# A cross-attention kernel on one core: the fourth batch's K projected ahead of V, its stack sent in halves

## What is computed

```python
Q = (query @ Wq.T + bq).reshape(B, Sq, N_HEADS, D_K).transpose(0, 2, 1, 3)
K = (key_value @ Wk.T + bk)...
V = (key_value @ Wv.T + bv)...
scores = jnp.einsum('bhqd,bhkd->bhqk', Q, K) / np.sqrt(D_K)
attn = jax.nn.softmax(scores, axis=-1)
context = jnp.einsum('bhqk,bhkd->bhqd', attn, V)
x = context @ W_o.T + b_o + query
return (x - mu) / jnp.sqrt(var + LN_EPS) * ln_gamma + ln_beta
```

## Time and profile before

| what | value |
|---|---|
| median of 3 runs | 149.05 us (148.85 to 150.97) |
| the profiled execution's own time | 149.44 us |
| its span, first to last instruction | 147.6 us |
| mean granted TensorE clock | 0.979 |
| PE busy | 131.0 us, 89% of the span |
| DVE, ACT, POOL busy | 94.0, 89.0, 82.3 us |
| DMA queue of SP (q1) | 17.36 MB, 36.9% of 16 engines |
| DMA queue of POOL (q0) | 1.70 MB, 4.6% |

### The profile page before, as it was taken

The page is one execution under the profiler, slowest core; times in us unless marked ns, Lnnn a source line. Parts: engine busy times, 40 slices in busy tenths (PEclk is TensorE's granted clock), DMA queues, the critical chain, the costliest instruction groups (busy, mean ns, idle before and its releaser), DMA issues.

```text
span 147.6 us, 3918 instructions
## 1 busy us (share of the span) xinstructions
PE 131.0 (89%) x1479; PEld 115.3 (78%) x1479; DVE 94.0 (64%) x220; ACT 89.0 (60%) x180; POOL 82.3 (56%) x101
## 2 busy tenths in 40 slices
PE   5798988799999269999999999999999999999940
PEld 4497967789889157988898989898989888778620
DVE  3466997988657333487657776877677786521432
ACT  3676445376586511957586678764867557776510
POOL 8958993984068400400429998991347007587531
PEclk9999999999999969999999999999999999999996
DMA  4996893780079896065007105641070010110111
GB/s 125 348 351 225 264 331 118 281 272 7 4 200 239 251 251 176 24 237 165 8 0 262 53 8 158 217 163 32 8 288 25 12 29 4 31 29 15 33 31 31
DMA packets 15731, 19.59 MB, mean 133 GB/s; under 512 B 2544, under 2 KB 14896, under 8 KB 15712
## 3 DMA queue, kind: packets, MB, share of 16 engines
q1 hardware_dynamic: 14656, 17.36, 36.9%
q0 software_dynamic: 592, 1.70, 4.6%
q10 hardware_dynamic: 464, 0.28, 0.6%
HBM read 6.30 MB, written 0.92 MB: 49 GB/s over the span
## 4 chain that ended last, share of the span: by engine, by line
PE 66%; SPq 14%; DMA 9%; DVE 3%; issue 2%; ACT 2%; ACTq 1%; POOLq 0%; DVEq 0%
PE m_bank L848 16%; PE st_bank L922 13%; PE pv_bank L938 13%; PE mx_bank L889 12%; SPq L259 6%; SPq L311 6%; DMA k_stack<-k_hl 5%; PE m_bank L969 4%; DMA c_raw<-ctxT 3%; PE m_bank L949 2%; DMA q_stack<-q_hl 1%; DVE mx L709 1%; PE m_bank L957 1%; PE mx_bank L922 1%; PE mx_bank L938 1%
## 5 line engine op out<-in xcount | busy, mean ns | idle before, releaser
L709 DVE TENSOR_REDUCE mx<-mx_bank 112x1 f32<-112x375 f32 x128 | 64.2, 541 | 26.1 <-PE mx_bank L889 25.9
L610 ACT ACTIVATE pw<-st_bank 125x448 f32<-125x448 f32 x90 | 47.6, 545 | 27.0 <-PE st_bank L922 26.8
L889 PE MATMUL mx_bank<-k_stack,q_stack 128*112 128x376 f32 x128 | 43.9, 356 | 6.0 <-DMA k_stack<-k_hl 4.1
L922 PE MATMUL st_bank<-q_stack,k_stack 128*125 128x224 f32 x180 | 36.3, 287 | 0.8 <-DMA q_stack<-shift_half 0.6
L922 PEld LDWEIGHTS st_bank<-q_stack,k_stack 128*125 128x125 f32 x180 | 29.8, 188 | 4.4 <-issue 2.6
L889 PEld LDWEIGHTS mx_bank<-k_stack,q_stack 128*112 128x112 f32 x128 | 22.3, 178 | 8.9 <-DMA k_stack<-k_hl 4.3
L411 POOL TENSOR_TENSOR k_hl<-k_full,k_hl 128x376 fp32r<-128x376 f32 x10 | 10.0, 999 | 25.5 <-ACT k_hl L528 25.5
L938 PE MATMUL pv_bank<-pw,v_sb 125*17 125x112 f32 x720 | 21.2, 264 | 0.0
L385 POOL TENSOR_TENSOR c_hl<-c_raw,c_hl 128x752 fp32r<-128x752 f32 x6 | 10.8, 1801 | 14.7 <-ACT c_hl L499 14.7
L938 PEld LDWEIGHTS pv_bank<-pw,v_sb 125*17 125x17 f32 x720 | 16.6, 99 | 3.1 <-issue 1.8
L848 PE MATMUL m_bank<-w_hl,c_hl 128*125 128x256 f32 x126 | 18.1, 282 | 0.0
(11 more groups left out here) (107 smaller groups left out, 170.4 us busy)
## 6 DMA issues: line engine op xcount, KB each, us to landing
k_stack<-k_hl SPq DMA_DIRECT2D x48, 188.0 KB, 2.5
c_raw<-ctxT SPq DMA_DIRECT2D x8, 375.0 KB, 3.9
q_stack<-q_hl SPq DMA_DIRECT2D x12, 112.0 KB, 2.3
q_stack<-q_hl SPq DMA_DIRECT2D x6, 168.0 KB, 3.3
x_space<-x_nat POOLq DMA_DIRECT2D x1, 896.0 KB, 11.7
out<-yo SPq DMA_DIRECT2D x8, 112.0 KB, 2.0
pw<-wT SPq DMA_DIRECT2D x2, 256.0 KB, 4.6
x_space<-xT SPq DMA_DIRECT2D x2, 224.0 KB, 5.5
```

Of the source, the lines that this page charges most:

```text
L610: nc.scalar.activation(p_tile[0:KC, n % PR, :, :], st_of(n)[0:KC, 0:4 * Q].rearrange("p (j q) -> p j q", j=4), ACT.Exp, scale=float(DK) ** ...
L709: nc.vector.tensor_reduce(mx[b % 2][:, h % 2, q_pair(h // 2):q_pair(h // 2) + 1], mx_bank[n % MR][0:Q, 0:KV], axis=AX_X, op=ALU.max, negat ...
L889: nc.tensor.matmul(mx_bank[n % MR][0:Q, 0:KVP], q_stack[k][:, side, q_pair(h // 2), b - Q_STACKS[k][0], :], k_stack[b % 3][:, h // 2, :], ...
L922: last = nc.tensor.matmul(st_of(n)[0:KC, k * 2 * Q:(k + 1) * 2 * Q], k_stack[i % 3][:, 2 * g + k, c * KC:(c + 1) * KC], q_stack[qk][:, :, ...
```

## The change

In batch 0, K of batch 3 is projected in units 2 and 4, V of batch 2 in units 5, 6 and 7, Q's third group in units 9 and 10. The taking of each by ACT and DVE moves with it, as do the orders of the PSUM banks. ACT splits context 4 in unit 8 and not in 5, and POOL does `context_lo(4)` behind the two `subtract_k`, not ahead of them. SP sends K's stack of batch 3 in batch 0: half 0 ahead of batch 1's shift, once batch 0 has done 6 units, half 1 behind the shift, once it has done 12; Q's third group follows. In batch 1, units 6 and 7 take no head for the maxima and units 8 to 11 take 1, 2, 2 and 1, where each of units 6 to 11 took one.

```diff
 U_OUT, U_OT, U_BIAS, U_Q, U_CONTEXT = 0, 6, 0, 11, 5
-U_K = ((9, 11), (8, 10))
-U_V = (2, 3, 4)
+U_K = ((2, 4), (8, 10))
+U_V = ((5, 6, 7), (2, 3, 4))
...
-FIRST_JOBS = {1: (("MT", 0, 1),), 5: (("Q", 2, 0),), 6: (("Q", 2, 1),)}
+FIRST_JOBS = {1: (("MT", 0, 1),), 9: (("Q", 2, 0),), 10: (("Q", 2, 1),)}
...
-M0_JOBS = [("K", 0, 0), ("V", 0, 0), ("Q", 1, 0), ("K", 2, 0), ("V", 2, 0), ("Q", 2, 0), ("K", 3, 0)]
-M1_JOBS = [("K", 0, 1), ("V", 0, 1), ("Q", 1, 1), ("K", 2, 1), ("MT", 0, 1), ("V", 2, 1), ("Q", 2, 1), ("MT", 1), ("K", 3, 1)]
+M0_JOBS = [("K", 0, 0), ("V", 0, 0), ("Q", 1, 0), ("K", 2, 0), ("K", 3, 0), ("V", 2, 0), ("Q", 2, 0)]
+M1_JOBS = [("K", 0, 1), ("V", 0, 1), ("Q", 1, 1), ("K", 2, 1), ("MT", 0, 1), ("K", 3, 1), ("V", 2, 1), ("MT", 1), ("Q", 2, 1)]
...
-FIRST_HEADS = ((2, 2, 2, 2, 2, 2, 2, 2, 1, 1, 1, 1), (2, 2, 2, 2, 2, 2, 1, 1, 1, 1, 1, 1))
+FIRST_HEADS = ((2, 2, 2, 2, 2, 2, 2, 2, 1, 1, 1, 1), (2, 2, 2, 2, 2, 2, 0, 0, 1, 2, 2, 1))
...
-                if b >= 3:
+                if b == 3:
+                    sp.wait_ge(st_full, HALF * (t + 1))
+                elif b > 3:
                     sp.wait_ge(st_full, UNITS * (b - 2))
...
             for i in range(B):
-                if 1 <= i < B - V_AHEAD:
+                if 2 <= i < B - V_AHEAD:
                     for t in range(2):
                         stack_k(i + V_AHEAD, t)
                 if i + AHEAD + 2 < B:
                     load_context(i + AHEAD + 2)
+                if i == 0:
+                    stack_k(AHEAD, 0)
                 if i + 1 < B:
                     stack_shift(i + 1)
+                if i == 0:
+                    stack_k(AHEAD, 1)
                 if i in (0, 3):
...
-                if i + AHEAD + 1 < B:
+                if 1 <= i and i + AHEAD + 1 < B:
                     context_lo(i + AHEAD + 1)
                 if i + AHEAD < B:
                     for t in range(2):
                         subtract_k(i + AHEAD, t)
+                if i == 0:
+                    context_lo(AHEAD + 1)
...
-                    if i + V_AHEAD < B and u in U_V[1:]:
-                        v_part(i + V_AHEAD, u - U_V[1])
-                    if i == 0 and u in (5, 6):
-                        q_hi_part(2, u - 5)
+                    if i + V_AHEAD < B and u in U_V[min(i, 1)][1:]:
+                        v_part(i + V_AHEAD, u - U_V[min(i, 1)][1])
+                    if i == 0 and u in (9, 10):
+                        q_hi_part(2, u - 9)
...
-                    if u == U_CONTEXT and i + AHEAD + 1 < B:
+                    if u == (U_CONTEXT if i else 8) and i + AHEAD + 1 < B:
                         context_hi(i + AHEAD + 1)
...
-                    if u in (6, 7) and i == 0:
-                        q_lo_part(2, u - 6)
+                    if u in (10, 11) and i == 0:
+                        q_lo_part(2, u - 10)
...
-                    if i + V_AHEAD < B and u in U_V:
-                        v_project(i + V_AHEAD, U_V.index(u))
+                    if i + V_AHEAD < B and u in U_V[min(i, 1)]:
+                        v_project(i + V_AHEAD, U_V[min(i, 1)].index(u))
```

## The result

The changed kernel takes 151.92 us (median of 20 runs, 149.91 to 155.36), the kernel before 149.21 (20 runs, 147.49 to 152.38). The ratio is 1.0159, with a 95% interval of 1.0116 to 1.0202: slower by 1.6%, where 2% faster was forecast. The time lies above the stated range. Every ratio here compares the fast executions of the two kernels, those within 1.5% of their fastest, so it differs from the quotient of the medians beside it. The profiled execution took 150.49 us with a span of 148.7, 1.1 more than before.

The account below looks back on a forecast made before the run. PE was taken to set the time from 60 us on, after a 4.11 us hole waiting for K's stack. Gain 5.65 less 0.65, less 1.85 for Q, leaves 3.15: 146.3 us profiled, median 145.9, range 143.8 to 148.3.

Parts of the forecast that it names:

- What bounds the kernel, what is bought: Batch 1, unit 6 to unit 9's first head: 4.6 us against 10.6, a gain of 5.65 if nothing makes PE wait.
- What batch 0 loses: Reordered PE work and later exponentials in batch 0 make batch 1 run 0.65 to 0.7 us later, leaving net 5.0.
- What comes late next: Q's third group now lands last: side 1 at 55.5, so head 49 in batch 1 starts there, not at 53.65.
- The bytes: SP's queue must move 1.61 MB from about 43.1, at 105 GB/s beside POOL's 149: side 1 lands at 55.8.
- The sum: Of the 5.0 us, 1.85 is given back at head 49 and 3.15 stays, with the clock priced at 0.
- C: Q's wait replaces K's and is longer, side 1 landing from 57.5 on; at 58.5 the time is 150.5 us; chance 0.06.
- B: Heads 48 and 49 wait 2.6 us or more together and the clock falls again: gain 0.8, 148.2 us; chance 0.15.
- A: Q's stack is in time, with no wait: gain 5.0, median 144.05 us; chance 0.23.
- D: Unit 0 of batch 1 or 2 waits for its shift, the latter behind context 6: 147.1 us; chance 0.08.

Follow-up runs that it names:

- e3: Changed kernel with x_nat issued in batch 1 behind context 5's low part, and Q's third group ahead of K's half 1: 146.75 us, ratio 0.985.
- e13: Changed kernel with Q's third group ahead of K's half 1 and x_nat issued in batch 2 behind context 6's low part: 145.47 us, ratio 0.978.
- e1: Changed kernel with only x_nat's load moved, to batch 1 behind the low part of context 5: 147.37 us, ratio 0.987.
- e7: The kernel of e3 with SP sending batch 2's shift ahead of context 6: ratio 1.001 to the kernel before.
- e11: Changed kernel with Q's third group ahead of K's half 1 and x_nat between batch 1's two K subtractions: 145.29 us, ratio 0.988.
- e4: Kernel before with only x_nat's load moved, to batch 1 behind the low part of context 5: 149.07 us, ratio 0.989.
- e5: Changed kernel with POOL's whole group of loads held back until unit 1 of batch 1 has its scores: ratio 1.020.
- e8: Changed kernel with POOL's group of loads moved ahead of the low part of context 4: ratio 1.031.
- e2: Changed kernel with only SP's order changed, Q's third group ahead of half 1 of K's stack: 151.77 us, ratio 1.020.
- e10: Kernel before with x_nat issued behind POOL's memset: 150.07 us, ratio 0.995.

## Why the prediction was wrong

*What bounds the kernel, what is bought.* Right, by e3 and e13: with the stack and Q in time, the hole and the half clock go. From unit 6 to the first head of unit 9 e13 takes 4.5 us (50.84 to 55.32), and 4.6 was forecast. e13's ratio of 0.978 is 3.3 us of the 5.0 that were priced for no wait at all, and its span is 3.4 below that of the kernel before. But its profiled execution was late before any of the change can act: ACT's exponential of unit 2 in batch 0, at 30.13 in the earlier trace rows, comes at 31.94. From that exponential to the end e13 is 5.2 us shorter, so the price of 5.0 was right in size, as far as one pair of profiled executions shows. Why the first 30 us differ from one execution to the next was not looked into.

*What batch 0 loses.* Right wherever it was read: PE's wait at unit 4 grew by 0.4 us, from 0.20 to 0.60, the maxima's transpose was forecast for 38.6 and came at 38.81, batch 1's unit 0 for 41.8 and came at 41.92 (41.39 before), unit 8 for 51.5 and came at 51.52. K's half 0 was issued at 33.74 (forecast 33.6) and landed by 38. Batch 1's shift took 1.8 us to land, and it did not make unit 0 wait.

*What comes late next.* Right in kind: Q's third group replaced K's stack, and POOL's loads moved forward to just the forecast times (41.99 and 44.39). The step that failed is "The bytes", with its last sentence on side 0. It gave each queue a constant rate (149 and 105 GB/s) and let Q's two sides land in proportion to the bytes ahead of them: side 1 at 55.5, side 0 "0.52 MB earlier, 51 to 53". Side 0 landed at 56.7 and side 1 at 58.7. The mean rate of SP's queue was not the error. It moved 1.69 MB between 43.1 and 56.75:

```profile
q1 hardware_dynamic: 984, 1.69, 48.2%
q0 software_dynamic: 464, 1.52, 43.8%
```

That is 124 GB/s. The forecast, 1.61 MB from 43.1 to 55.8, is 127. All of POOL's loads were moved in the same time. What was wrong is which bytes moved when, and for whom the last ones were. In 48.5 to 51.5 us it looked like this:

```profile
q0 software_dynamic: 142, 0.57, 67.4%
q1 hardware_dynamic: 61, 0.14, 13.5%
```

x_nat was being drained and Q hardly moved. Side 0's last DMA, issued 0.9 us behind x_nat, landed with side 1's, 0.8 us behind the first of them. And by 56.75 SP's queue had moved more than the 1.61 MB that the forecast counted for side 1, which landed 2 us later still: some of what moved was context 5, issued behind it. So the parts of a transfer did not finish in proportion to the bytes ahead of it. That this is a matter of how unequal the 16 engines' backlogs are is a guess, as the profile does not tell them apart. A mean rate over a window of the kernel before could not show it, as there Q had been sent with nothing of POOL ahead of it. What the earlier trace rows showed for 46 to 52.84, 60.4% against 32.2%, is a mean of two things. Mostly beside `wo` and the three rows both queues moved, 0.38 and 0.35 MB in 48 to 51 us; in 51 to 53 us, when what POOL's queue moved was mostly x_nat, SP's got little:

```profile
q0 software_dynamic: 104, 0.39, 77.5%
q1 hardware_dynamic: 88, 0.11, 19.0%
```

The prediction took the mean for a constant rate.

*The sum.* The forecast had 1.85 us of wait and no clock price. Measured were 4.82 us and a window of 3.71 at a mean clock of 0.55. By the prediction's own terms: 5.0 less 4.82 less 1.6 is -1.4, and the span grew by 1.1.

*Rivals.* C was nearest, in price and in sign: decisive from a landing of 57.5 on, and 150.5 us at 58.5. Side 1 landed at 58.7, with a median of 151.92. Its chance of 0.06 was too low. But its reason, SP's queue at 105 GB/s or less, was not what happened (124 GB/s), and PE's wait was for side 0, at head 48, and not for side 1. What spoke against it ("they are through by 54 to 56") was nearly true of POOL's queue, whose last load landed at 57.5, and did not help the transfers behind it. B was part of it: the clock did fall. A, no wait at all, was reached only with x_nat moved and Q ahead of K's half 1 (e13). D did not come in the changed kernel: batch 2's shift landed 6.7 and 7.4 us behind its issues, and PE did not wait for it. In the experiments it was right as a hint and wrong in its cause: in e1, e3 and e7 batch 2's shift was late beside x_nat, not behind context 6 (e7), and with x_nat 3 us behind it (e11) it was in time.

*The parts of the change.* Projecting K early and sending half 0 ahead of the shift does what it says. e1 has it and waits 1.5 us for its stacks where e4 without it waits 3.1. The loss is made by two side effects: Q goes out 4.1 us later (44.03 for 39.88) and POOL's loads 2.3 us earlier (41.99 for 44.27), so that they cross. e5 shows that undoing the second alone, by holding the loads back 3 us, gives nothing back, and e1 that it takes getting x_nat past Q. That Q at its old time in the changed kernel would be free of it was not tried: its projection ends too late.

## What to carry to other kernels

When a transfer is moved, list what is issued on all queues in the 5 us around its new place, and ask for each pair which goes out first: a large load of no urgency that goes out ahead of an urgent transfer delays it by microseconds (Q's side 0 landed 3.6 us later with x_nat ahead of it than in e1), and neither a mean rate nor the load's own deadline shows it. A small urgent DMA suffers as well as a large one. Price a late arrival with the clock behind it too: here 4 us of hole were followed by more than 3 us at half clock in both kernels.

## What the runs showed of the hardware

- Across two queues, a large load held up what was issued behind it and hardly what was issued ahead of it. With x_nat (896 KB) issued 1.6 us ahead, two DMAs of 7 KB took 6.4 and 7.3 us instead of 1.8, and SP's queue got no packet in 4 us (e8). In e7, of two such DMAs 0.6 us apart, with x_nat issued between them, one landed 3.1 and the other 6.9 us behind its issue.
- The issue of a DMA can be held up as well: Q's third took 1.93 us on SP instead of 0.6. x_nat is not needed for it. In the kernel before, the fifth DMA of a K stack took 1.44 us at 63.84, with nothing of POOL's issued for 17 us, and in e5 the fourth took 2.08 at 64.83. In all three several DMAs of SP's had not landed yet. Whether that is the queue filling up was not tried.
- In batch 1 and at batch 2's unit 0, waits of 0.9 and 0.6 us (e1), 1.4 (e3) and 2.8 (e7) left the granted clock at 1.00. Waits of 3.1 (e4), 4.1 (before) and 4.8 us (changed) were each followed by some 3 us with a stretch at 0.50, and waits of 3.6 (e5), 4.0 (e2) and 5.3 us (e8) by almost 7. The length of one wait does not decide it: e10's 2.6 us at head 48 was followed by a stretch at 0.50 as well, and the same wait of 1.87 us near 27.4 was followed by one in e7 and by none in e3. e7's window:

```profile
28.58:31.99 3.41, 3.41 (x14) 0.50 0.82 249
```
